# Attention layers of a two-layer kernel: the global layer's causal mask on GpSimd after the exponential, and five steps moved

## The chip, the cores and the metric

One core of one Trainium2 chip runs the whole program. The metric is the device time of one execution in microseconds (us); the kernel before took 745.13 us in the median of three runs (745.00 to 746.87). Engines are called as in the profile: PE is TensorE's matrix product (PEld its weight load), DVE is VectorE, ACT is ScalarE, POOL is GpSimd, SP is SyncE.

## The reference, cut to what matters

The input x is 8 sequences of 256 tokens of 128 numbers. Level 0 adds a two-directional Mamba block and a mixture of experts; level 1 adds an attention block and a second mixture of experts. The change lies in level 1's attention block, which is two layers one after the other:

```
x = x + global_latent_attn(rmsnorm(x, norm1_w), ...)   # causal mask
x = x + local_gqa_attn(rmsnorm(x, norm2_w), ...)       # causal, and within 32 tokens
# in each: 16 query heads, 4 key heads of 8 numbers; q, k rotated (rope), then
qk_norm(x) = x * rsqrt(mean(x * x, -1) + EPS)          # per head
scores = where(mask, q k^T / sqrt(8), -1e30); probs = softmax(scores); out = probs v
```

## The kernel before, in words

The program runs its stages one behind the other: level 0 to about 500 us, routing and experts of level 1 to about 565 us, then the attention stage (`attention_timeline`, lines 234 to 275) to the end at 742 us. Only that stage is touched.

**Units.** A sequence of one layer has three blocks of 128 keys by 128 queries, in the order `BLOCKS` = (0,0), (1,1), (0,1) as (key tile, query tile); a block is two units, each of two key heads, so that 16 sequence-layers give 96 units: 0 to 47 the global layer, 48 to 95 the local one. For a unit PE multiplies keys by queries into two PSUM banks (`scores`, L2133, or L2130 for the local corner blocks of 32 columns), ACT takes the exponential of 1024 columns into `probs` (`exps`, L1121), and once per block, two units, PE multiplies `probs` by the values (`average(t)`, L2160 or L2157). On the diagonal blocks (0,0) and (1,1) the mask is added on PE ahead of the scores: four 64-row products of an identity with a table of 0 and -30000 (L2122), which start the sum in PSUM. `scores(U)` waits until the exponential of unit U-2 has freed its banks; `probs` has three buffers.

**Preparation.** Tokens come in groups G of two sequences, four for each layer (G = 0 to 7), and a group is 12 units. Its steps are: rms (ACT squares L1031, DVE sum and variance L1481 and L1483, POOL's power -0.5 L702, DVE scaling L1489), T (PE transposes L1983, ACT copy L1034), L (latent product, global layer alone, L1978, ACT copy L1038), Q (PE L1989, DVE rotation L1543, L1545), K (PE L1987, DVE L1553 to L1565, the last of which writes `qk`), sqr (ACT squares `qk` L1042, DVE sum and variance L1570, L1574), inv (ACT logarithm and exponential L1045, L1048, DVE scaling L1577), split (ACT and DVE write float16 pairs, L1053, L1055, L1581, L1584), and behind the attention O1 and O2 (output transposes and product, ACT copy L1059, DVE sum L1588). Three turns for each sequence bring keys (part 0) and the two tiles of queries (parts 1 and 2) into the layout that the scores read: PE L2042 or L2048 into one bank, DVE copy L1625 or L1627. After its last average a sequence is copied by ACT (L1128), turned back by PE (L2168) and divided by its sums on DVE (`head_out`, L1659, L1665).

**Order.** Every engine runs its queue strictly in order, and all four queues are written from one list: `put(slot, event)` places an event at a slot number, one slot for each unit. PE's order in a slot is the events in the order of placing, then the unit, then the average. The others take turns, T, L and O1 first, then the unit, then the rest. The slots before the change are those of the removed lines of the diff; relative to 12G, and so modulo 12: Q 1, K 3, sqr 4, inv 5, split 6, rms 7, O1 7, O2 9, T 10, L 0; turns 9, 10, 0 and 3, 4, 6. POOL has nothing in this stage but the six powers.

Of the kernel before, what the change touches and what calls it, by code (L numbers as in the profile page):

```python
# [19 lines left out]
ALU = mybir.AluOpType  # L20
# [3 lines left out]
P = 128  # L24
# [77 lines left out]
    "turn_q", "turn_copied", "scores_ready", "probs_ready", "av_done", "den_done",  # L102
# [131 lines left out]
def attention_timeline():  # L234

    slots = {}

    def put(at, *ev):
        slots.setdefault(at, []).append(ev)

    for b in range(2 * SEQS):
        for part, at in enumerate((-3, -2, 0)):
            put(6 * b + at + (b == 0 and part == 2), "turn", b, part)
        put(6 * b + 10, "back", b)
        put(6 * b + 8, "copy", b)  # L260
    for G in range(GROUPS):
        for name, at in (("rms", -17), ("T", -14), ("L", -12), ("Q", -11), ("K", -9), ("sqr", -8), ("inv", -7), ("split", -6),
                         ("O1", 19), ("O2", 21)):
            if name != "L" or G < GROUPS // 2:
                put(12 * G + at, name, G)
    order, readers = [], []
    for at in range(min(slots), max(slots) + 1):
        here = slots.get(at, [])
        unit = [("unit", at)] if 0 <= at < UNITS1 else []
        if at % 2 and 1 < at <= UNITS1 + 1:  # L270
            unit.append(("average", at // 2 - 1))
        first = [ev for ev in here if ev[0] in ("turn", "T", "L", "O1")]
        order += here + unit
        readers += first + unit + [ev for ev in here if ev not in first]
    return order, readers
# [18 lines left out]
PREP = {ev: n for n, ev in enumerate(ev for ev in FILL + AT_ORDER if ev[0] in ("T", "L", "Q", "K", "O1", "O2"))}  # L294

# [73 lines left out]
def build(nc, a, out):  # L369
    with ExitStack() as ctx:  # L370
# [164 lines left out]
        def after(eng, name, count):  # L535

            if not (isinstance(count, int) and count <= 0):
                eng.wait_ge(sem[name], count)
# [109 lines left out]
        def _(pool):  # L648
# [135 lines left out]
            pool.memset(v_ring[:, :, :, :, VPAD + HD:VPAD + HD + 1], 1.0).then_inc(sem["ones_ready"], 1)  # L784
            for ev in FILL[1:] + AT_READERS:
                if ev[0] == "rms":
                    rms_pow(ev[1])


        @block.scalar  # L790
        def _(act):
# [226 lines left out]
            def prepare(ev):  # L1018
# [5 lines left out]
                if kind == "rms":  # L1024
# [14 lines left out]
                elif kind == "sqr":  # L1039
                    act.wait_ge(sem["roped"], G + 1)  # L1040
                    after(act, "qk_sum", G)
                    act.activation(qk_sqr[:], qk[:, r].rearrange("p h d -> p (h d)"), ACT.Square).then_inc(sem["qk_sq"], 1)  # L1042
# [97 lines left out]
        def _(dve):  # L1140
# [386 lines left out]
            def prepare(ev):  # L1527
# [8 lines left out]
                if kind == "rms":  # L1536
                    rms_sums(G)
                    rms_scale(G)
                elif kind == "Q":
# [27 lines left out]
                elif kind == "sqr":  # L1567
                    dve.wait_ge(sem["qk_sq"], G + 1)
# [114 lines left out]
        def _(pe):  # L1683
# [422 lines left out]
            def scores(U):  # L2106
# [8 lines left out]
                for kv in kvs:  # L2115
# [3 lines left out]
                    elif kt == qt:  # L2119
                        for rows in HALF_ROWS:  # L2120
                            keys = rows if kv == kvs[0] else HALF_ROWS[rows is HALF_ROWS[0]]
                            pe.matmul(ps[keys, kv], ident16[rows, rows],  # L2122
                                      masks[rows, l if kv == kvs[0] else 3 + l].unsqueeze(1).broadcast_to([P // 2, GROUP, P]),
                                      start=True, stop=False)
                if t % 3 < 2:
                    pe.wait_ge(sem["turn_copied"], TURN["turn", b, 1 + t % 3] + 1)
                for kv in kvs:
# [4 lines left out]
                    else:  # L2132
                        last = pe.matmul(ps[:, kv], kT[g, r, kt * P:(kt + 1) * P], qT[g, r, :, qt * P:(qt + 1) * P],  # L2133
                                         start=(kt != qt), stop=True)
                last.then_inc(sem["scores_ready"], 1)

            def average(t):
# [5 lines left out]
                pe.wait_ge(sem["probs_ready"], 2 * t + 2)  # L2143
                if t % 3 == 0:
                    pe.wait_ge(sem["v_ready"], b // 2 + 1)
# [125 lines left out]
```

## Time and profile before

| what | us |
|---|---|
| median of 3 runs | 745.13 |
| the profiled execution's own time | 744.09 |
| its span | 742.3 |
| attention stage, about 565 to 742.3 | 177 |
| ACT exponentials L1121, 96 | 86.5 busy |
| PE averages L2160, 640 products | 43.9 busy |
| POOL in the whole span | 418.6 busy, nearly all before 520 |

The page has the span in 40 slices of 18.6 us: in the attention stage PE is busy 8 or 9 tenths, ACT 6 or 7, DVE 5 or 6, POOL nothing to speak of. A busy PE is not PE at its peak, as its products overlap. Rows of the chain of waits are "start us, us, what"; rows of the timeline are "start us, duration us, engine, line, operation, output<-input, shapes, count", with idle time before the row and who ended it in brackets.

### The profile page before, as it was taken

How to read it: one execution, taken by the hardware profiler on the slowest of the kernel's cores; microseconds unless marked ns; L12 is line 12 of the kernel's file. 1: busy time of each engine (PE TensorE's matmuls, PEld its weight loads, DVE VectorE, ACT ScalarE, POOL GpSimd, SP SyncE). 2: the span in 40 equal slices, each digit the busy share in tenths (PEclk: the TensorE clock that was granted, in tenths of full speed). 3: DMA queues.
4: the chain of work that ended last, by engine and by line, in shares of the span. 5: the costliest groups of instructions: out<-in, count | busy, mean ns of one | idle time of the engine just before them, and what ended most of it. 6: DMA issues, size and time to landing. Idle time of an engine off the chain costs nothing.

```text
span 742.3 us, 14099 instructions
## 1 busy us (share of the span) xinstructions
PE 639.4 (86%) x4851; PEld 468.8 (63%) x4851; DVE 581.2 (78%) x852; ACT 526.4 (71%) x1001; POOL 418.6 (56%) x362
## 2 busy tenths in 40 slices
PE   5899987879889799798997985888999888989896
PEld 3488965657668577576675764876877344445443
DVE  6535769999999999999999999997316556566552
ACT  3455465896978969878789899673544777866673
POOL 5400047999999999999999999992000000000000
PEclk9699999999999999999999998999999999999998
DMA  6313467669688596885877858781110000000000
GB/s 210 114 58 115 147 145 219 208 160 262 182 201 252 158 239 198 183 253 169 193 260 157 250 181 195 228 230 43 57 58 1 2 1 1 2 1 2 15 16 29
DMA packets 81415, 100.18 MB, mean 135 GB/s; under 512 B 32561, under 2 KB 37817, under 8 KB 81345
## 3 DMA queue, kind: packets, MB, share of 16 engines
q1 hardware_dynamic: 81344, 99.29, 48.2%
q8 instruction: 39, 0.64, 0.3%
q14 instruction: 32, 0.25, 0.1%
HBM read 96.12 MB, written 3.24 MB: 134 GB/s over the span
## 4 chain that ended last, share of the span: by engine, by line
PE 50%; DVE 17%; issue 14%; ACT 13%; POOL 4%; DMA 0%; POOLq 0%; DVEq 0%; ACTq 0%
PE ps L1849 5%; DVE hc L1222 4%; DVE ps L1214 4%; PE ps L1827 3%; DVE moe L1214 3%; PE ps L2160 3%; PE ps L1904 3%; PE ps L1919 3%; PE ps L1759 2%; PE ps L1810 2%; PE ps L2133 2%; PE ps L2057 2%; PE ps L2067 2%; PE ps L1779 2%; POOL drive L689 2%
## 5 line engine op out<-in xcount | busy, mean ns | idle before, releaser
L689 POOL TENSOR_TENSOR drive<-dtu,b_sb 128x512 f32<-128x512 f32 x160 | 204.1, 1285 | 1.5 <-DMA b_sb<-bc_rows 1.4
L697 POOL TENSOR_TENSOR hc<-moe,c_sb 128x512 f32<-128x512 f32 x128 | 166.1, 1298 | 8.2 <-DVE moe L1214 8.2
L1214 DVE TENSOR_TENSOR_SCAN moe<-ps,drive 128x512 f32<-128x512 f32 x128 | 153.3, 1198 | 0.7 <-ACT decay_sb L885 0.5
L1849 PE MATMUL ps<-ident,hc 128*128 128x128 f32 x1024 | 134.9, 275 | 3.3 <-POOL hc L697 3.0
L1849 PEld LDWEIGHTS ps<-ident,hc 128*128 128x128 f32 x1024 | 116.6, 142 | 28.6 <-issue 19.3
L885 ACT ACTIVATE ps<-dt,negA 128x510 f32<-128x510 f32 x160 | 106.5, 677 | 28.9 <-DVE moe L1214 28.2
L1214 DVE TENSOR_TENSOR_SCAN ps<-decay_sb,ps 128x512 f32<-128x512 f32 x96 | 117.1, 1220 | 1.2 <-ACT decay_sb L885 1.1
L1121 ACT ACTIVATE probs<-ps 128x1024 f32<-128x1024 f32 (+1 forms) x96 | 86.5, 916 | 35.6 <-PE ps L2133 29.3
L702 POOL TENSOR_TENSOR stat<-stat,halfc 128x4 f32<-128x4 f32 x7 | 7.1, 1008 | 170.8 <-DVE stat L1483 170.8
L1222 DVE TENSOR_TENSOR hc<-ps,c_sb 128x512 f32<-128x512 f32 x128 | 85.2, 666 | 0.0
L885 ACT ACTIVATE decay_sb<-dt,negA 128x510 f32<-128x510 f32 x96 | 68.3, 711 | 16.0 <-DVE ps L1214 16.0
L1827 PE MATMUL ps<-xm,dtuT 128*128 128x128 f32 x384 | 53.1, 282 | 11.4 <-DVE hc L1222 11.4
L916 ACT ACTIVATE scaled<-dtuT,bT 128x128 f32<-128x128 f32 x192 | 60.0, 389 | 0.6 <-PE ps L1829 0.6
L1827 PEld LDWEIGHTS ps<-xm,dtuT 128*128 128x128 f32 x384 | 47.4, 194 | 15.3 <-issue 15.3
L1829 PE MATMUL ps<-ident,scaled 128*128 128x128 f32 x192 | 30.1, 280 | 27.9 <-DVE hc L1222 27.9
L1829 PEld LDWEIGHTS ps<-ident,scaled 128*128 128x128 f32 x192 | 21.9, 144 | 35.3 <-issue 26.2
L2160 PE MATMUL ps<-probs,v_all 128*32 128x256 f32 x640 | 43.9, 393 | 0.0
L1214 DVE TENSOR_TENSOR_SCAN ps<-ps,drive 128x512 f32<-128x512 f32 x32 | 39.1, 1222 | 2.0 <-ACT ps L885 2.0
L775 POOL TENSOR_TENSOR seqstat<-seqstat,halfc 128x2 f32<-128x2 f32 x8 | 5.6, 700 | 58.3 <-DVE seqstat L1412 58.3
L820 ACT ACTIVATE hT<-ps,wbuf 128x256 f32<-128x256 f32 x64 | 25.8, 476 | 16.2 <-PE ps L1904 16.2
L1627 DVE CAST qT<-ps 128x512 f16<-128x512 f32 x32 | 22.0, 689 | 17.3 <-PE ps L2048 17.1
L1919 PEld LDWEIGHTS ps<-wbuf,hT 128*128 128x128 f32 x256 | 30.8, 192 | 3.1 <-issue 2.5
(282 smaller groups left out, 1191.0 us busy)
## 6 DMA issues: line engine op xcount, KB each, us to landing
b_sb<-bc_rows SPq DMA_DIRECT2D x128, 256.0 KB, 4.2
c_sb<-bc_rows SPq DMA_DIRECT2D x128, 256.0 KB, 4.1
xm<-spot_rows SPq DMA_DIRECT2D x48, 256.0 KB, 4.9
wbuf<-in_pack SPq DMA_DIRECT2D x16, 514.0 KB, 3.5
wbuf<-in_pack SPq DMA_DIRECT2D x8, 512.0 KB, 5.5
spot_rows<-c_sb SPq DMA_DIRECT2D x6, 256.0 KB, 3.6
x_sb<-in_x SPq DMA_DIRECT2D x4, 256.0 KB, 3.8
out<-x_sb SPq DMA_DIRECT2D x4, 256.0 KB, 2.3
```

Source lines behind the costliest of these rows:

```text
L689: pool.tensor_tensor(drive_of(N, half), dtu[:, N // STATES % 2, half], b_sb[:, N % B_RING], ALU.mult) \
L697: pool.tensor_tensor(hc[:, 2 * (N % DEEP) + half], h_of(q), c_sb[:, N % C_RING], ALU.mult).then_inc(sem["hc_pooled"], 1)
L885: act.activation(seqs(decay_bank(q))[:, :, lo:lo + SEQ - 1], seqs(dt[:, g % 2, half])[:, :, lo:lo + SEQ - 1], ACT.Exp, scale=negA[:, g // ...
L916: last = act.activation(scaled[:, n % 2, block], dtuT[:, block], ACT.Copy, scale=bT[:, t, j:j + 1])
L1121: act.activation(probs[keys, t % 3, heads_u, 0:width], ps[keys, heads_u, 0:width], ACT.Exp, scale=HD ** -0.5).then_inc(sem["probs_ready"], 1)
L1214: dve.tensor_tensor_scan(h_of(q)[:, turn], decay_bank(q)[:, turn], source[:, turn], 0.0, ALU.mult, ALU.add).then_inc(sem["scan_done"], 1)
L1222: dve.tensor_tensor(hc[:, 2 * (N % DEEP)], h_of(q), c_sb[:, N % C_RING], ALU.mult).then_inc(sem["hc_ready"], 1)
L1827: last = pe.matmul(ps[:, H_BANKS[N % OWN_H], block], dtuT[:, block], spots[:, n % SPOT_RING, block], start=True, stop=True)
L1829: last = pe.transpose(ps[:, H_BANKS[N % OWN_H], block], scaled[:, n % 2, block], ident[:])
L1849: last = pe.matmul(ps[:, Y_BANK + half, block], hc[:, 2 * (N % DEEP) + half, block], ident[:], start=False, stop=True, is_transpose=True, ...
L1919: last = pe.matmul(bank[:, t * D:(t + 1) * D], hT[:, k, c, t * P:(t + 1) * P], wbuf[:, r, HIDDEN + CHUNKS + c * D:HIDDEN + CHUNKS + (c + 1 ...
L2160: last = pe.matmul(to, v, probs[:, t % 3, kv, pair * SEQ:(pair + 1) * SEQ], start=(t % 3 < 2 and pair == 0), stop=(t % 3 != 1 and pair == 1))
```

## The change

The causal mask of the global layer's diagonal blocks (32 units, `by_pool`) leaves PE; POOL instead zeroes the hidden entries of `probs` after the exponential, in place, with one `affine_select` over 128 x 1024 (`hide`), and `average` waits for a new signal, `probs_seen`. The local layer keeps its masks. `average(t)` comes one unit later (behind unit 2t+4 instead of 2t+3), and so the copy and turn back of a sequence (9 and 11 for 8 and 10), O1 and O2 (20 and 22 for 19 and 21). The third turn of a sequence comes one slot sooner (-1 for 0). For groups 2 to 7 rms becomes two events: squares, with the DVE sum and variance, at the old slot, and root, two slots later, in which ACT (logarithm, then exponential of -0.5 times it) computes what POOL's power did, and DVE scales; T comes one slot later (-13 for -14). The squares of `qk` (sqr) are taken by DVE, as a product of `qk` with itself, instead of by ACT.

```diff
-        for part, at in enumerate((-3, -2, 0)):
-            put(6 * b + at + (b == 0 and part == 2), "turn", b, part)
-        put(6 * b + 10, "back", b)
-        put(6 * b + 8, "copy", b)
+        for part, at in enumerate((-3, -2, -1)):
+            put(1 if (b, part) == (0, 2) else 6 * b + at, "turn", b, part)
+        put(6 * b + 11, "back", b)
+        put(6 * b + 9, "copy", b)
     for G in range(GROUPS):
-        for name, at in (("rms", -17), ("T", -14), ("L", -12), ("Q", -11), ("K", -9), ("sqr", -8), ("inv", -7), ("split", -6),
-                         ("O1", 19), ("O2", 21)):
+        for name, at in (("T", -13), ("L", -12), ("Q", -11), ("K", -9), ("sqr", -8), ("inv", -7), ("split", -6),
+                         ("O1", 20), ("O2", 22)):
             if name != "L" or G < GROUPS // 2:
                 put(12 * G + at, name, G)
+        if G >= 2:
+            put(12 * G - 17, "squares", G)
+            put(12 * G - 15, "root", G)
+        else:
+            put(12 * G - 17, "rms", G)
...
-        if at % 2 and 1 < at <= UNITS1 + 1:
-            unit.append(("average", at // 2 - 1))
+        if at % 2 == 0 and 2 < at <= UNITS1 + 2:
+            unit.append(("average", at // 2 - 2))
...
+def by_pool(U):
+    return U // 6 < SEQS and BLOCKS[U // 2 % 3] != (0, 1)
...
+            def hide(U):
+                pool.wait_ge(sem["probs_ready"], U + 1)
+                p = probs[:, U // 2 % 3, 2 * (U % 2):2 * (U % 2) + 2].rearrange("p g (j q) -> p g j q", j=GROUP)
+                pool.affine_select(p, p, [[0, 2], [0, GROUP], [1, P]], ALU.is_ge, 0.0, base=0, channel_multiplier=-1) \
+                    .then_inc(sem["probs_seen"], 1)
...
+                if kind == "root":
+                    act.wait_ge(sem["rms_var"], G)
+                    act.activation(stat[:, 1, rows], stat[:, 2, rows], ACT.Ln).then_inc(sem["rms_ln"], 1)
+                    act.wait_ge(sem["rms_ln"], G - 1)
+                    act.activation(stat[:, 3, rows], stat[:, 1, rows], ACT.Exp, scale=-0.5).then_inc(sem["rms_pow"], 1)
...
-                elif kind == "sqr":
-                    act.wait_ge(sem["roped"], G + 1)
-                    after(act, "qk_sum", G)
-                    act.activation(qk_sqr[:], qk[:, r].rearrange("p h d -> p (h d)"), ACT.Square).then_inc(sem["qk_sq"], 1)
...
                 elif kind == "sqr":
+                    dve.wait_ge(sem["roped"], G + 1)
+                    qk_row = qk[:, r].rearrange("p h d -> p (h d)")
+                    dve.tensor_tensor(qk_sqr[:], qk_row, qk_row, ALU.mult).then_inc(sem["qk_sq"], 1)
                     dve.wait_ge(sem["qk_sq"], G + 1)
...
-                    elif kt == qt:
+                    elif kt == qt and not by_pool(U):
...
-                                         start=(kt != qt), stop=True)
+                                         start=(kt != qt or by_pool(U)), stop=True)
...
                 pe.wait_ge(sem["probs_ready"], 2 * t + 2)
+                after(pe, "probs_seen", seen_before(2 * t + 2))
```

`seen_before(n)` counts the units below n that are POOL's.

## Rows read from the trace of the kernel before

**Rows 1.** Busy time by stretch, K product to K product (us, engines' busy time, PEclk, DMA).
```profile
591.93:614.69 22.76, 20.64 (x217) 10.27 (x215) 13.29 (x27) 17.28 (x24) 1.01 (x1) 1.00 0.01 1
614.69:636.56 21.87, 19.73 (x216) 10.31 (x214) 13.29 (x27) 16.67 (x23) 1.01 (x1) 1.00 0.01 2
636.56:658.22 21.66, 19.51 (x214) 10.08 (x213) 13.29 (x27) 16.59 (x23) 1.01 (x1) 1.00 0.01 1
658.22:680.00 21.78, 21.08 (x233) 11.91 (x231) 13.73 (x28) 15.41 (x24) 1.01 (x1) 0.92 0.01 2
```

**Rows 2.** Chain of waits, 604 to 615 us: start, us, engine, output, line.
```profile
604.38 1.02 POOL stat L702
...
607.10 0.66 PE ps L1983 x4
607.75 0.33 PE ps L2133 x4
608.08 1.00 PE ps L2160 x16
...
609.41 0.97 PE ps L1978 x2
...
611.06 1.16 PE ps L1989 x8
612.22 0.34 PE ps L2122 x4
...
614.76 1.03 PE ps L1987 x8
```

**Rows 3.** Timeline, one group from K to split, 592 to 602 us.
```profile
591.93 1.10 PE L1987 MATMUL ps<-w_kvu,latT 32*128 32x64 f32 x8
...
593.86 0.82 DVE L1565 TENSOR_TENSOR qk<-rot 128x640 f32<-128x640 f32 x1
...
596.53 0.49 DVE L1665 TENSOR_TENSOR moe<-ps,den 128x128 f32<-128x128 f32 x2
...
596.79 0.73 ACT L1042 ACTIVATE qk_sqr<-qk 128x640 f32<-128x640 f32 x1
...
597.55 0.82 DVE L1570 TENSOR_REDUCE norm<-qk_sqr 128x80 f32<-128x640 f32 x1 [0.53 <-ACT qk_sqr L1042]
...
598.64 0.27 ACT L1045 ACTIVATE norm<-norm 128x80 f32<-128x80 f32 x1 [0.21 <-DVE norm L1574]
...
599.24 0.82 DVE L1577 TENSOR_TENSOR qk<-qk,norm 128x640 f32<-128x640 f32 x1 [0.64 <-ACT norm L1048]
...
599.98 0.68 DVE L1627 CAST qT<-ps 128x512 f16<-128x512 f32 x1
...
600.42 1.04 ACT L1055 ACTIVATE qs<-qk 128x1024 f16<-128x1024 f32 x1
```

**Rows 4.** Timeline of ACT from the split to the second next exponentials.
```profile
601.37 0.58 ACT L1059 ACTIVATE xmT<-ps 128x512 f32<-128x512 f32 x1
...
602.75 0.63 ACT L1031 ACTIVATE sq<-xn 128x512 f32<-128x512 f32 x1
...
607.79 0.69 ACT L1034 ACTIVATE xmT<-ps,cols 128x512 f32<-128x512 f32 x1 [2.10 <-PE ps L1983]
...
608.38 1.93 ACT L1121 ACTIVATE probs<-ps 128x1024 f32<-128x1024 f32 x2
```

**Rows 5.** POOL by line and form: count, busy us, mean ns, idle before.
```profile
L689 POOL TENSOR_TENSOR drive<-dtu,b_sb 128x512 f32<-128x512 f32 x160 | 204.1, 1285 | 1.5 <-DMA b_sb<-bc_rows 1.4
...
L782 POOL MEMSET v_all<- 128x1040 f32 x1 | 1.0, 960 | 0.0
```

**Rows 6.** Timeline near 15 us, the program's start: DVE, then POOL.
```profile
13.01 0.69 DVE L1188 TENSOR_TENSOR xn<-xm,stat 128x512 f32<-128x512 f32 x1
...
15.58 1.75 DVE L1188 TENSOR_TENSOR xn<-xm,stat 128x512 f32<-128x512 f32 x1 [1.08 <-POOL stat L735]
...
15.51 1.27 POOL L670 TENSOR_TENSOR w_tap<-dtu,w_in 128x512 f32<-128x512 f32 x1
```

More of the change, by code:

```diff
@@ L101 @@
     "rope_a", "roped", "v_ready", "qk_sq", "qk_sum", "qk_var", "qk_ln", "qk_inv", "qk_normed", "qk_hi", "qk_split",
-    "turn_q", "turn_copied", "scores_ready", "probs_ready", "av_done", "den_done",
+    "turn_q", "turn_copied", "scores_ready", "probs_ready", "probs_seen", "rms_ln", "av_done", "den_done",
     "ones_ready", "av_copied", "av_turned", "heads_done", "out_ready",
@@ L294, with seen_before @@
 PREP = {ev: n for n, ev in enumerate(ev for ev in FILL + AT_ORDER if ev[0] in ("T", "L", "Q", "K", "O1", "O2"))}
+def by_pool(U):
+    return U // 6 < SEQS and BLOCKS[U // 2 % 3] != (0, 1)
+def seen_before(U):
+    return sum(by_pool(V) for V in range(U))
 def shared_before(q):
@@ L787, in _ @@
                     rms_pow(ev[1])
+                elif ev[0] == "unit" and by_pool(ev[1]):
+                    hide(ev[1])
         @block.scalar
@@ L1023, in prepare @@
                 rows = slice(GT * k, GT * k + GT)
-                if kind == "rms":
+                if kind == "root":
[3 more added lines that the diff above has]
+                    act.activation(stat[:, 3, rows], stat[:, 1, rows], ACT.Exp, scale=-0.5).then_inc(sem["rms_pow"], 1)
+                elif kind in ("rms", "squares"):
                     if l:
@@ L1538, in prepare @@
                     rms_scale(G)
+                elif kind == "squares":
+                    rms_sums(G)
+                elif kind == "root":
+                    rms_scale(G)
                 elif kind == "Q":
```

## The prediction, made before the changed kernel ran

> **What bounds the kernel now.** I read the page's slices first: the change touches nothing before about 565 us, so only the last 177 us count. Then I cut that stage by groups, from one K product to the next [rows 1]. A group takes 21.7 to 22.8 us, PE is busy in some 19.5 to 20.6 of them, ACT in 16.6 to 17.3, DVE in 13.3, POOL in 1.0. No engine fills the period. So I read the chain of waits [rows 2] and the timeline [rows 3, 4] to see how a group goes round, with the K product at 591.93 as zero:
>
> - K to norm: K product, DVE's rotation, whose last sum ends at +2.75; ACT squares `qk` only at +4.86, as its queue has exponentials ahead; DVE's sum follows at +5.62, ACT's logarithm at +6.71, DVE's scaling (L1577) ends at +8.13 [rows 3].
> - norm to T: ACT splits until +9.53, copies for O1, and squares the next group's tokens at +10.82 [rows 3, 4]; POOL's power ends at +13.47, DVE scales, copies keys and adds O2, and T starts at +15.17 [rows 2].
> - T to K: here PE is packed. Its rows follow each other without a gap to the next K product at +22.76 (614.69 in the window's bound) [rows 1, 2]: 7.59 us, three masks of 0.34 among them.
>
> The bound is therefore this ring through four in-order queues. PE alone sets only its last third.
>
> **Masks off PE.** 32 units lose four products each, 0.34 us a unit [rows 2]: 10.9 us of PE in all. Of the eight in a period of 12 units only the three between T and K lie on PE's packed stretch (1.0 us). The other five stand between K and T, where PE waits for ACT and DVE; there I cost them at nothing, since the split and the exponentials cover them. If that cover were gone, they would be worth 1.7 us a group.
>
> **Squares of `qk` on DVE.** Removed: 0.73 us of ACT. Added: one product over 640 elements with two SBUF inputs, as L1565, 0.82 us [rows 3]. DVE no longer waits for ACT's queue. Its queue from +2.75 is: copy of the second turn 0.6, squares 0.82, sum and variance 1.1 (598.64 less 597.55), copy of the third turn 0.6 (now ahead of the scaling, since that turn is a slot sooner), `head_out` 0.85 (reciprocal and the 0.49 row), scaling 0.82. That puts the scaling's end at about +7.47 for +8.13: a gain of 0.65. The logarithm and exponential are hidden behind the third turn's copy and `head_out`.
>
> **Root on ACT, two slots later.** Removed: POOL's 1.02 [rows 2] and DVE's wait for it. Added on ACT: two small operations of 0.27 each (as L1045), 0.57 with the handover. But they stand behind more of ACT's queue. From the scaling's end at +7.47: split to +8.79, exponential 0.93 (two took 1.93 less the overlap [rows 4]), squares 0.55, O1 copy 0.53, two exponentials 1.86, sequence copy 0.55, root 0.57: +13.8. Then DVE's scaling, a copy of the second turn and the O2 sum; in the old order scaling, key copy and O2 sum took 1.70 (607.10 less the power's end), here 1.97, as the turn's copy is 0.27 longer. T starts at +15.75 instead of +15.17. So moving the root costs what the faster norm gives, and 0.6 more; it is repaid because unit 10 and its average are by then already done.
>
> **T to K after the change.** T 0.58, unit 11; L must wait for T's copy, which ends 1.38 after T's start (607.79 + 0.69) [rows 4], since the average that used to lie between now comes behind unit 0: L at +1.43. Then L 0.97, unit 0 0.33, average 1.00, Q 1.09, units 1 and 2 side by side 0.33 (as the pair at 607.75), average 1.00, keys' turn 0.22, sum 6.37 for 7.59 [rows 2]. The period is 15.75 + 6.37 = 22.1 for 22.76: minus 0.65.
>
> **The sum without any contact between POOL and DVE.** First slots, two masks ahead of the first K: -0.7. K1 to K2 and K2 to K3: -0.65 each. K3 to K4 has no L, so Q waits for unit 0 and an average only: 15.75 + 4.87 = 20.6 for 21.87, -1.25. K4 to K5 ends in the local layer with its masks: 15.75 + 6.2 = 21.95 for 21.66, +0.3. The two local periods: +0.2 each. Behind the last K: -0.3. Together -2.8 us. The average, the copy and O1, O2 a unit later cost nothing more: behind unit 95 no unit follows, so PE's order of the last two averages is the same work.
>
> **POOL's selects, and what they meet.** The trace has no `affine_select`. Below lies the write-only row, 960 ns for 1040 elements; above lies twice the two-input row, 2.57 us for 1024 [rows 5]. I take 1.3 us: a select reads 1024 values from SBUF, as many as the two inputs of the 1285 ns row have together, and the read count is what separates those rows. Eight of them are 10 us of a 22 us period, so POOL keeps up; at 2.57 it would be 20.6 and just not. As latency they are hidden: `average` runs about two us after the second exponential of its block is done, and where a select ends later (unit 3's, at most 1.5 us) PE has slack between K and T. Queued behind that wait on PE are the next unit's scores, and ACT's exponential behind them.
>
> What is not hidden is contention. It shows at the start of the program [rows 6]: DVE's product over 512 elements with both inputs in SBUF takes 0.69 alone, and 1.75 when POOL's L670 (15.51 to 16.78) started 0.07 earlier: it stood until POOL was done and then took its 0.67. The ring has five such DVE steps between K and T on its critical side: rotation sum, the new squares, scaling of `qk`, key pairs, scaling of tokens; query pairs too. With POOL busy nearly 0.5 of the time I laid selects of length p beside the steps above, each side waiting for the other to finish: T comes later by 0.45 us for p = 1.0, 1.65 for p = 1.25, 3.25 for p = 1.5. A plain mean (busy share times half a select, over five to seven steps) gives 0.9, 1.4 and 2.0. I take +1.7 a period, in four periods with selects: +6.8.
>
> The Trainium skill, "SBUF — State Buffer", section "Who interferes with whom", says the same as a rule: a VectorE instruction with two SBUF inputs and a GpSimd one that reads SBUF exclude each other, the later one waiting in full. The 1.75 us row agrees [rows 6]. It speaks against this change, which adds both kinds. The skill's "GPSIMD Engine Reference", section "Performance pitfalls for Q7 kernels", gives compare-and-select loops 1.03 to 2.03 cycles an element; worked out at its 1.2 GHz that is an estimate of 0.88 to 1.73 us for a select, and by its two ends the sum would be near -2 or beyond +9 us; no row here shows it.
>
> **Forecast.** -2.8 + 6.8 = +4.0 on the profiled 744.09 (span 742.3 and 1.8 around it), so 748.1; the median lies 1.04 above the profiled run: 749.1.
>
> **Rivals.** (1) *The selects slip between DVE's steps* (short select, or phases that fall well): +0.45 x 4 - 2.8 = -1.0, no measurable change, 744.1. For it: DVE is busy in only 13.3 of 22.8 us [rows 1]. Against: selects become ready right behind exponentials, and DVE's steps come from the same ring. (2) *PE's relief counts in full.* If the masks outside T to K hold up ACT too, because scores wait for the exponential two units back and ACT then starves, the eight masks give 2.7 us a period and the first slots 0.7, less some contention: 4 x (-2.7 + 0.6) + 0.7 x -1 = about -9; half of it, -5, I take as its time: 740. For it: PE is busy for 20.6 of 22.76 us [rows 1]. Against: between K and T it is ACT and DVE that the chain follows. (3) *TensorE's clock.* In 658 to 680 the granted clock was 0.92 instead of 1.00 [rows 1], in a stretch where PE had lighter work than in the groups before, whose clock was full. The engine drops to its lower level (1.2 instead of 2.4 GHz) for part of that stretch. With masks gone the global groups grow light as well; a dip costs one to two us when it falls between T and K, four of them +6: 751. (4) *A select near 2.57 us*: POOL becomes the bound, periods go beyond 25 us, 758 or more. (5) *The mask leaves PE but the queue of PE waits in `average` instead*: every select is then on the path, the same 1.3 us that the 0.34 x 2 saved, +0.6 for each of 16 blocks, +10 less 3: 752; slack of two us speaks against it.
>
> **How the numbers follow.** Forecast, contention above the gain (747.5 to 753): 0.38; clock or waiting `average` on top, or the long select: 0.10; rival 1, within 0.3%: 0.20; rival 2 and anything faster: 0.32. 0.3% is 2.2 us, about what a measurement of this kernel tells from no change. That gives faster 0.32, within 0.20, slower 0.48. The range takes rival 2's middle at its low end and the long contention case at its high end: 739.5 to 756. The forecast's own range is 747.5 to 753.
>
> **What the profile of after would show.** Selects: their mean ns on POOL, and how many DVE rows of L1565, the new squares, L1577, L1581, L1489 are longer than 0.82, 0.82, 0.82, 0.42, 0.69. Right: several of them stretched by up to a select's length, periods K to K of 23 to 24 us in the global layer. Wrong by rival 1: durations as before, periods 22. Wrong by rival 2: periods near 20 and ACT idle for less than 4 us in each. The scaling L1577 should end about 7.5 us (plus contention) behind K, T start 15.75 or later, L wait for T's copy. A granted clock under 1.00 before 655 us would be rival 3, PE waiting for POOL ahead of L2160 rival 5.

## The result, and the profile after

The changed kernel took 750.92 us in the median of five runs (749.38 to 750.96), the kernel before beside it 745.0: a ratio of 1.0071 with a 95% interval of 1.0053 to 1.0090, so slower by more than 0.3%. The forecast of 749.1 had the sign and nearly the size. The profiled execution took 749.38, with a span of 747.7.

First the same cuts as [rows 1], from K product to K product, for the whole attention stage (us, then busy time of PE, PEld, DVE, ACT, POOL, then the mean granted clock, DMA share, GB/s):

```profile
571.45:595.39 23.94, 17.27 (x167) 8.33 (x167) 16.59 (x25) 15.88 (x24) 11.42 (x9) 0.86 0.00 1
595.39:617.60 22.21, 17.56 (x184) 9.20 (x182) 14.79 (x28) 16.80 (x25) 9.56 (x9) 1.00 0.01 1
617.60:638.97 21.37, 17.57 (x182) 9.72 (x181) 14.79 (x28) 16.42 (x24) 9.72 (x9) 0.92 0.01 2
638.97:663.18 24.21, 20.66 (x195) 11.69 (x195) 14.75 (x28) 16.74 (x24) 8.01 (x7) 0.86 0.01 1
663.18:684.88 21.70, 19.70 (x223) 11.41 (x222) 13.83 (x28) 13.52 (x24) 0.00 (x0) 0.92 0.00 1
684.88:707.59 22.71, 20.84 (x223) 11.85 (x222) 14.52 (x29) 14.13 (x24) 0.00 (x0) 0.85 0.05 13
707.59:747.70 40.11, 32.54 (x396) 17.73 (x394) 18.88 (x40) 22.50 (x34) 0.00 (x0) 0.94 0.07 21
```

The kernel before has seven such stretches too. Four of them [rows 1] do not hold, as the last window there, 658.22 to 680.00, is not from K to K. The third stands there with a bound of 636.56, where K starts at 636.39, so that it takes 21.70 us and not 21.87. These five are:

```profile
570.40:591.93 21.53, 18.39 (x200) 8.41 (x198) 13.95 (x24) 16.55 (x23) 1.01 (x1) 1.00 0.00 1
614.69:636.39 21.70, 19.56 (x214) 10.14 (x213) 13.29 (x27) 16.50 (x23) 1.01 (x1) 1.00 0.01 2
658.06:678.99 20.93, 20.23 (x222) 11.12 (x221) 13.31 (x27) 14.56 (x23) 1.01 (x1) 0.92 0.01 2
678.99:701.40 22.41, 20.47 (x223) 10.84 (x221) 13.91 (x28) 14.45 (x23) 1.01 (x1) 0.92 0.05 14
701.40:742.30 40.90, 33.47 (x396) 18.32 (x394) 18.27 (x39) 23.13 (x35) 0.00 (x0) 0.93 0.07 21
```

From the first K to the end: 176.1 us after, 171.9 before. The loss isn't spread as forecast. Two stretches carry it: the first, 23.94 for 21.53, and the fourth, 24.21 for some 21.7. The second is 0.55 us shorter than before (22.76 [rows 1]), the third 0.3 (21.70). And the granted clock, at its full 1.00 in the global layer before, is now 0.86, 0.92 and 0.86 in three of four stretches: TensorE ran for part of them at 1.2 instead of 2.4 GHz. A stretch of mean clock c holds half clock for 2 (1 - c) of its length. By that estimate it is about 27 us ahead of the last K against about 7 before (17 against 0 in the global layer's four stretches, 10 against 7 in the two local ones), and 32 against 13 with the last stretch.

Next, from the changed kernel's timeline, the cycle that begins with K at 595.39 (start, duration, engine, line, operation, shapes, idle time before and who ended it):

```profile
597.66 1.48 POOL L804 TENSOR_SCALAR_AFFINE_SELECT probs<-probs 128x1024 f32<-128x1024 f32 x1 [0.15 <-ACT probs L1146]
598.70 1.11 DVE L1599 TENSOR_TENSOR qk_sqr<-qk 128x640 f32<-128x640 f32 x1
...
602.21 0.81 DVE L1609 TENSOR_TENSOR qk<-qk,norm 128x640 f32<-128x640 f32 x1
...
607.25 0.38 PE L2080 MATMUL ps<-ident,qs 128*128 128x128 f16 x4 [1.48 <-DVE kT L1657]
...
609.01 0.99 DVE L1514 TENSOR_TENSOR xm<-xn,stat 128x512 f32<-128x512 f32 x1 [1.91 <-ACT stat L1052]
...
611.25 0.66 PE L2015 MATMUL ps<-ident,xm 128*128 128x128 f32 x4
```

The scaling of `qk` ends at +7.63 (forecast +7.47, plus contact), T starts at +15.86 (forecast +15.75), the next K comes at +22.21 (forecast 22.1 without contact, 23.8 with it). DVE's 1.91 us of waiting for ACT's root is the new wait that the later root was said to bring; PE stands idle for 1.48 us before the second turn. No wait of PE for POOL ahead of an average, the sign of rival 5, is in the trace.

Then the prices of contact, each line's instructions over the whole span (ns: shortest, median, longest):

```profile
L804 POOL TENSOR_SCALAR_AFFINE_SELECT probs<-probs x32: 1094/1097/3145, 569.9 to 651.9; 128x1024 f32<-128x1024 f32 x32
L1599 DVE TENSOR_TENSOR qk_sqr<-qk x8: 814/964/1111, 534.7 to 710.8; 128x640 f32<-128x640 f32 x8
L1613 DVE TENSOR_TENSOR ks<-qk,ks x8: 415/586/1012, 562.1 to 715.3; 128x256 f16<-128x256 f32 x8
L1514 DVE TENSOR_TENSOR xm<-acc,stat x4: 692/838/987, 631.2 to 698.1; 128x512 f32<-128x512 f32 x4
L1709 DVE TENSOR_TENSOR x_sb<-x_sb,sq x1: 3115/3115/3115, 571.6 to 571.6; 128x2048 f32<-128x2048 f32 x1
```

A select takes 1.10 us alone, not the 1.3 I took: it reads as many values as the two-input row of 1.28 us, so the read count alone does not set the length. It stretches the squares by 0.3 us, `ks` by up to 0.6, the token scaling by 0.3. The last row is a step that I had not looked at: the sum of the first residual, once, in the first cycle, 3.12 us for 2.28 before. What follows it in that cycle of the changed kernel:

```profile
571.52 5.82 POOL L804 TENSOR_SCALAR_AFFINE_SELECT probs<-probs 128x1024 f32<-128x1024 f32 x3 [0.49 <-ACT probs L1146]
571.64 3.12 DVE L1709 TENSOR_TENSOR x_sb<-x_sb,sq 128x2048 f32<-128x2048 f32 x1
...
577.14 0.38 PE L2080 MATMUL ps<-ident,qs 128*128 128x128 f16 x4 [2.94 <-DVE qT L1659]
```

Both sides wait: three selects take 5.82 us instead of 3.3, the sum 0.83 us more, and PE stands for 2.94 us before the third turn, whose predecessor's copy is queued behind the sum on DVE.

Last, PE in the fourth stretch, in the middle of a time at half clock:

```profile
651.16 2.02 PE L2021 MATMUL ps<-w_o,xmT 128*128 128x128 f32 x8
...
653.65 1.94 PE L2193 MATMUL ps<-probs,v_all 128*32 128x256 f32 x16
```

At full clock the same groups take 1.11 and 1.07 us: with the neighbours, some 2.4 us for this one dip (a dip is a time at half clock).

### The profile page after: what moved, and what is told of

It reads as the page before. It is cut to its first block, busy times and chain, and to the rows that moved or that the text cites. A ratio compares the mean times of both kernels' runs of the same rounds, so it can differ in the third digit from the quotient of the medians.

```text
span 747.7 us, 13951 instructions
## 1 busy us (share of the span) xinstructions
PE 632.3 (85%) x4723; PEld 468.9 (63%) x4723; DVE 590.9 (79%) x860; ACT 523.0 (70%) x1005; POOL 452.5 (61%) x388
## 4 chain that ended last, share of the span: by engine, by line
PE 52%; DVE 19%; issue 11%; ACT 11%; POOL 4%; SPq 1%; DMA 1%; DVEq 0%; POOLq 0%; ACTq 0%
PE ps L1881 6%; PE ps L2193 4%; DVE ps L1239 3%; PE ps L1936 3%; DVE hc L1247 3%; PE ps L1859 3%; PE ps L1951 3%; DVE moe L1239 3%; PE ps L2021 2%; PE ps L1791 2%; PE ps L1842 2%; POOL drive L704 2%; PE ps L2089 2%; PE ps L2099 2%; PE ps L1811 2%
## 5 line engine op out<-in xcount | busy, mean ns | idle before, releaser
L804 POOL TENSOR_SCALAR_AFFINE_SELECT probs<-probs 128x1024 f32<-128x1024 f32 x32 | 39.8, 1258 | 74.2 <-ACT probs L1146 74.1
L2193 PE MATMUL ps<-probs,v_all 128*32 128x256 f32 x640 | 46.3, 410 | 0.0
L2165 PE MATMUL ps<-qT,kT 32*128 32x512 f16 x160 | 28.9, 397 | 5.7 <-ACT probs L1146 4.2
```

The source lines that it names most:

```text
L2193: last = pe.matmul(to, v, probs[:, t % 3, kv, pair * SEQ:(pair + 1) * SEQ], start=(t % 3 < 2 and pair == 0), stop=(t % 3 != 1 and pair == 1))
```

## Experiments

The theory after the result: three things of different kinds add up. (a) The ring gains about what the no-contact sum said. (b) Contact with the selects takes back less than forecast. (c) The rest is half clock and the first cycle's sum. Rivals to it: contact alone; the order of the moved steps.

Diffs are against the changed kernel where nothing else is said.

### Parts of the change, undone or alone

**both_masks**: the masks stay on POOL, and TensorE adds them as well.

```diff
-                    elif kt == qt and not by_pool(U):
+                    elif kt == qt:
...
-                                         start=(kt != qt or by_pool(U)), stop=True)
+                                         start=(kt != qt), stop=True)
```

> The changed kernel with the four mask products of each diagonal block put back on PE as well, so that POOL still runs its 32 selects and PE has its old work. In the changed kernel's trace PE's clock stands at half for 27 us of the attention stage, in the kernel before for 7. If the clock is the cost, the global layer's dips go, and the time falls although PE has 10.9 us more to do: 746 to 748 against 750.9. If the contact of POOL with DVE is the cost, it stays or rises by what PE's added work takes: 751 to 754.

753.24 us, 1.0114 of before (1.0086 to 1.0143): 2.3 us over the change, with intervals that overlap by a little. The half clock ahead of the last K fell only from about 27 to 24 us, but not evenly: in the global layer, where the masks went back, from 17 to 10, while the local layer, whose work this edit leaves alone, had 14 for 10. So the mask products are partial cover, and they cost time of their own. That cost is read where the clock is full in both, in the second stretch:

```profile
595.83:619.64 23.81, 20.99 (x217) 10.42 (x215) 15.03 (x28) 16.94 (x25) 9.21 (x9) 1.00 0.01 1
```

It took 22.21 in the changed kernel: the relief of PE is worth 1.6 us there, of the 2.7 that eight masks are long.

**masks_back**: no selects at all, every mask by TensorE; the moved steps stay.

```diff
-    return U // 6 < SEQS and BLOCKS[U // 2 % 3] != (0, 1)
+    return False
```

> The changed kernel with all masks on PE and no select; every moved step stays moved. If POOL's contact with DVE or the lighter PE is the cost, this is at or under the kernel before: 742 to 746. If the moved steps are the cost (root behind two more exponentials, T a slot later), it stays at 749 to 751.

747.54 us, 1.0031 (1.0014 to 1.0048), between the two expected ranges. Four of its stretches:

```profile
595.30:618.20 22.90, 20.88 (x216) 10.41 (x214) 13.84 (x28) 16.79 (x25) 0.00 (x0) 1.00 0.01 1
639.60:660.90 21.30, 19.74 (x215) 10.26 (x213) 13.84 (x28) 16.14 (x24) 0.00 (x0) 1.00 0.00 1
660.90:683.30 22.40, 20.84 (x222) 11.56 (x221) 13.84 (x28) 13.44 (x24) 0.00 (x0) 0.85 0.01 1
683.30:706.50 23.20, 21.20 (x223) 12.29 (x221) 14.54 (x29) 14.19 (x24) 0.00 (x0) 0.85 0.05 13
```

The moved steps alone lose some 2.4 us, in two places. One is the first stretch, 23.3 for 21.5. The other is the local layer, where at a clock of 0.85 the two stretches take 22.4 and 23.2 for 20.9 and 22.4. The three global stretches in between, at full clock, take 22.9, 21.4 and 21.3 for 22.8, 21.7 and 21.7, and the last 39.8 for 40.9, which gives part of it back. With all masks on PE the global layer has about 3 us of half clock, all in the first stretch.

**masks_alone**: the kernel before, with the selects and with averages, copy, turn back, O1 and O2 a unit later; rms, T, third turn and squares as they were. The diff is against the kernel before and leaves out the selects, which are as in the change.

```diff
-        put(6 * b + 10, "back", b)
-        put(6 * b + 8, "copy", b)
+        put(6 * b + 11, "back", b)
+        put(6 * b + 9, "copy", b)
...
-                         ("O1", 19), ("O2", 21)):
+                         ("O1", 20), ("O2", 22)):
...
-        if at % 2 and 1 < at <= UNITS1 + 1:
-            unit.append(("average", at // 2 - 1))
+        if at % 2 == 0 and 2 < at <= UNITS1 + 2:
+            unit.append(("average", at // 2 - 2))
```

**old_root**: the changed kernel with masks by TensorE and rms and T in their old slots, with POOL's power.

```diff
-        for name, at in (("T", -13), ("L", -12), ("Q", -11), ("K", -9), ("sqr", -8), ("inv", -7), ("split", -6),
+        for name, at in (("rms", -17), ("T", -14), ("L", -12), ("Q", -11), ("K", -9), ("sqr", -8), ("inv", -7), ("split", -6),
...
-        if G >= 2:
-            put(12 * G - 17, "squares", G)
-            put(12 * G - 15, "root", G)
-        else:
-            put(12 * G - 17, "rms", G)
...
-    return U // 6 < SEQS and BLOCKS[U // 2 % 3] != (0, 1)
+    return False
```

> The kernel before with the masks by POOL and the averages, copies, turns back, O1 and O2 a unit later, nothing else moved. POOL's power then queues behind selects and DVE waits for it. If the masks part is the slow one: 750 or more. If the moved steps are: at or under the kernel before, 742 to 746.

> All masks on PE, no selects, and the rms steps back as they were: POOL's power in one event at the old slot, T at -14. What stays moved is the squares of qk on DVE, the third turn a slot sooner and the averages a unit later. By the ring of the prediction the norm comes 0.65 us a group sooner and the root's 0.6 us loss goes, so this is 743 to 745 and under masks_back (747.5) by 2 to 4 us. If the late averages are the cost, it stays at 747.

773.38 us, 1.0386 (1.0358 to 1.0413), and 774.37 us, 1.0384 (1.0370 to 1.0397); the second lies 27 us above anything that was expected. Both have periods of some 26 to 28 us as far as the last K. The timeline of old_root:

```profile
609.77 0.69 DVE L1509 TENSOR_TENSOR xm<-xn,stat 128x512 f32<-128x512 f32 x1 [1.12 <-POOL stat L712]
...
610.38 0.42 DVE L1652 CAST kT<-ps 128x256 f16<-128x256 f32 x1
...
610.95 0.59 PE L2075 MATMUL ps<-ident,qs 128*128 128x128 f16 x4 [2.95 <-DVE kT L1652]
...
611.33 2.02 PE L2016 MATMUL ps<-w_o,xmT 128*128 128x128 f32 x8
...
614.13 1.11 PE L2010 MATMUL ps<-ident,xm 128*128 128x128 f32 x4 [0.78 <-DVE acc L1615]
```

O2 a unit later falls into the slot of T at its old place (both in slot 10, modulo 12). DVE's key copy stands behind the scaling, which stands behind POOL's power; the second turn waits 2.95 us for it, and then O2, its sum and T follow one after the other at half clock (O2 2.02 us for 1.11). So the later root and T, moved together, are what makes the later averages possible at all: masks_back has them and takes 747.54. Which of the two it is, these runs don't part. The prediction took that move as costing 0.6 us, to be repaid; it had not seen what it prevents.

**squares_turn** (its diff is against the kernel before): the kernel before, with the squares of `qk` on DVE and the third turn a slot sooner.

```diff
-        for part, at in enumerate((-3, -2, 0)):
-            put(6 * b + at + (b == 0 and part == 2), "turn", b, part)
+        for part, at in enumerate((-3, -2, -1)):
+            put(1 if (b, part) == (0, 2) else 6 * b + at, "turn", b, part)
...
-                    act.activation(qk_sqr[:], qk[:, r].rearrange("p h d -> p (h d)"), ACT.Square).then_inc(sem["qk_sq"], 1)
...
+                    qk_row = qk[:, r].rearrange("p h d -> p (h d)")
+                    dve.tensor_tensor(qk_sqr[:], qk_row, qk_row, ALU.mult).then_inc(sem["qk_sq"], 1)
```

> The kernel before with two parts of the change alone: the squares of qk on DVE and the third turn a slot sooner. By the ring this is the gainful part: 0.65 us sooner in each of seven groups, 4 us at most, 741 to 743. If the order of the ring was read wrongly: 745.

751.43 us, 1.0072 (1.0059 to 1.0084), above both expected times. In its timeline, with K at 596.91:

```profile
600.10 0.39 PE L2047 MATMUL ps<-ident,qs 128*128 128x128 f16 x4
...
600.52 0.69 DVE L1626 CAST qT<-ps 128x512 f16<-128x512 f32 x1 [0.86 <-PE ps L2047]
...
601.92 0.82 DVE L1566 TENSOR_TENSOR qk_sqr<-qk 128x640 f32<-128x640 f32 x1
```

The squares start at +5.01, no sooner than ACT's at +4.86 [rows 3], and the scaling ends at +8.37 for +8.13. With the average still ahead of the second turn in PE's queue, DVE's copy waits for that turn and the squares wait behind the copy. In the changed kernel the average is later and the squares start at +3.31. So I read the 0.65 us a period that I gave to the squares' new engine as the work of that step and the late average together; no run has these two alone. Without the late average the two moves of this run lose 6 us. It isn't half clock: the global stretches behind the first take 23.2, 22.2 and 22.1 for 22.8, 21.7 and 21.7, all at 1.00.

### Contact

**write_only**: the select is replaced by a POOL operation that only writes; the mask of the global diagonal blocks is left out.

```diff
-                pool.affine_select(p, p, [[0, 2], [0, GROUP], [1, P]], ALU.is_ge, 0.0, base=0, channel_multiplier=-1) \
-                    .then_inc(sem["probs_seen"], 1)
+                if seen_before(U):
+                    pool.wait_ge(sem["probs_seen"], seen_before(U))
+                pool.memset(xnT[:, 0:1190], 0.0).then_inc(sem["probs_seen"], 1)
```

> The changed kernel with each select replaced by a fill of 1190 unused elements of SBUF, about as long (1.1 us) and waited for in the same way; it only writes, and the causal mask of the global layer is left out. If two readers exclude each other, DVE's rows are back at 0.82, 0.41 and 0.69 us, and the contact's price is what the time falls by: 1 us a group at most by the stretched rows, 4 to 5 us in all, 746 to 747. If the clock is the cost, dips stay and the time is 749 to 751.

748.52 us, 1.0054 (1.0030 to 1.0078), between the two expected ranges; that interval overlaps the change's. Its rows decide:

```profile
L1600 DVE TENSOR_TENSOR qk_sqr<-qk x8: 815/815/824, 533.1 to 705.1; 128x640 f32<-128x640 f32 x8
L1614 DVE TENSOR_TENSOR ks<-qk,ks x8: 415/426/426, 560.6 to 709.6; 128x256 f16<-128x256 f32 x8
L1710 DVE TENSOR_TENSOR x_sb<-x_sb,sq x1: 2282/2282/2282, 570.1 to 570.1; 128x2048 f32<-128x2048 f32 x1
```

Every stretched row is back at its own length, though POOL is busy for 8.7 us of a stretch (9.6 with selects). The stretch comes from a POOL operation that reads. The dips stayed: about 21 us of half clock in the global layer of the profiled execution, which was the fastest of the twelve (744.87), so contact doesn't cause them. Its second stretch is at full clock:

```profile
592.53:614.13 21.60, 17.55 (x185) 9.21 (x183) 13.84 (x28) 16.76 (x25) 8.73 (x9) 1.00 0.01 2
```

Between it and the 22.9 us of masks_back lie only the masks on PE and an operation on POOL that stretches nothing: without contact the relief is worth 1.3 us. And about 3 us of half clock in the global layer with masks (masks_back) against 21 without (write_only) says what brings most dips there: the masks' leaving. The mean clock over the whole span, 0.965 and 0.954 in the median of twelve executions each, agrees.

**add_late**: the changed kernel with the first residual's sum at unit 12 instead of 3. By then part of `sq` is overwritten, so the residual isn't the reference's.

```diff
-                elif ev == ("unit", 3):
+                elif ev == ("unit", 12):
```

> The changed kernel with DVE's 128 x 2048 sum into x_sb (3.12 us against 2.28 before, as POOL's select held it) moved from unit 3 to unit 12, where DVE waits 3.2 us for Q. The first period took 23.9 us against 21.5 before, with PE idle for 2.9 us behind that sum and half clock after it. If that sum is the cause of the first period, it falls to 21 to 22 us and the time by 1.5 to 3 us, to 748 to 749.5. If not, no change.

748.29 us, 1.0026 (1.0006 to 1.0047). The first stretch is 21.4 us instead of 23.9, at the same low clock (0.84 for 0.86), and the time is 2.6 us less: the sum is what lengthened that stretch.

**before_split** and **masks_back_split** move it without changing the result, in the kernel before and in masks_back: rows 8 to 12 at unit 3, the others at unit 12.

```diff
-                    dve.tensor_tensor(x_sb[:], x_sb[:], sq[:], ALU.add).then_inc(sem["x1_ready"], 1)
+                    dve.tensor_tensor(x_sb[:, 8:12], x_sb[:, 8:12], sq[:, 8:12], ALU.add).then_inc(sem["x1_ready"], 1)
+                elif ev == ("unit", 12):
+                    dve.tensor_tensor(x_sb[:, 12:16], x_sb[:, 12:16], sq[:, 12:16], ALU.add).then_inc(sem["x1_ready"], 1)
+                    dve.tensor_tensor(x_sb[:, 0:8], x_sb[:, 0:8], sq[:, 0:8], ALU.add).then_inc(sem["x1_ready"], 1)
```

> The kernel before with VectorE's addition of the first residual (2.28 us in front of the copy for the second turn in the first cycle) split: rows 8 to 12 of it at unit 3, the others at unit 12. If the in-order queue of VectorE hands this instruction to the first period one for one, the first K to K is 1.1 to 1.7 us shorter than its 21.5 and the time is 743 to 744. If the first period is set by the loads and weights, nothing moves: 745.

> The changed kernel with every mask by TensorE again (no select at all), and the same split of VectorE's addition. With all masks by TensorE and the addition whole it was 1.0031 of the kernel before. If the addition is what the moved steps lose, 745 to 746 us. If it is the dips or the order, 747 to 748 as it was.

745.04 us, 0.9987 (0.9972 to 1.0002), and 746.35 us, 1.0004 (0.9983 to 1.0024). Where the moved steps stand, the first stretch falls from 23.3 to 22.2 us; the two local ones stay at a clock of 0.85 and 22.5 and 23.2 us. In the kernel before it doesn't fall (21.7 for 21.5), so there the sum was hidden, and splitting it makes no faster kernel. The split run of before gives the price of a dip, as its order behind the first cycle is unchanged:

```profile
661.80:682.70 20.90, 18.97 (x223) 10.38 (x221) 13.30 (x27) 14.43 (x23) 1.01 (x1) 1.00 0.01 2
682.70:703.60 20.90, 18.96 (x223) 10.38 (x221) 13.91 (x28) 14.42 (x23) 1.01 (x1) 1.00 0.05 15
```

With a clock of 0.92 the kernel before took 20.93 and 22.41 for these two: the same mean clock cost nothing in one and 1.5 us in the other. It matters where the dip lies. And since the order is the same, dips also come and go from one execution of a kernel to the next; what one profile counts of them is one sample.

### The clock

**keep_busy**: seven needless products behind the scores of unit 9.

```diff
+                    if ev[1] % 12 == 9 and ev[1] < 12 * (GROUPS - 1):
+                        keep_busy(n)
```

> The changed kernel with seven needless products of 512 columns (0.21 us each) on PE behind the scores of unit 9 of every group of twelve, where PE stands idle for 1.3 to 1.5 us in each group before the second turn. They write the preparation bank before O2 or T overwrites it, and take nothing that another engine waits for. In the changed kernel half clock follows each such idle stretch (582 to 590, 630 to 634, 650 to 658 us). If the clock is what the missing masks cost, half-clock time goes from 27 us to under 10 and the time to 745 to 748. If the clock doesn't matter, 750 to 753.

750.44 us, 1.0058 (1.0040 to 1.0077), the time that was expected if the clock didn't matter. But the edit didn't do what it was for:

```profile
608.81 3.17 PE L2209 MATMUL ps<-masks,ident 128*128 128x512 f16 x7 [0.62 <-ACT xmT L1084]
```

The products wait for O1's copy, last 3.17 us and outrun the gap, and the half clock still is about 17 us ahead of the last K. So the run decides nothing about the clock.

**fill_gaps** puts them at two places, into banks that are free at that time (in this run `keep_busy(n, bank, count)` issues `count` products of the masks' first tile with the identity; `filled` is true for units below 84):

```diff
+                    if ev[1] % 12 == 9 and filled:
+                        keep_busy(n, AV_BANK + 1, 3)
...
+                    if ev[1] % 12 == 7 and filled:
+                        keep_busy(n, PREP_BANK, 5)
+                    if ev[1] % 12 == 9 and filled:
+                        keep_busy(n, AV_BANK + 1, 6)
```

> The changed kernel with products put into TensorE's idle stretches of every unit cycle but the last: five behind the scores of unit 7, three before and six behind those of unit 9, all of the masks' first tile with the identity, into banks that nobody reads then. If the stretches at half clock are what is left of the loss (27 us of them in the profiled run of the changed kernel, some 2.4 us for one of 6.8 us), the profile shows under 10 us of them behind the first K, periods of 21.3 to 22 us, and 745 to 747 us. If order and contact alone set the time, the products bring nothing or delay the unit behind them: 751 or more, with the dips or without.

745.72 us, 0.9998 (0.9983 to 1.0014). Its stretches:

```profile
571.00:594.00 23.00, 20.10 (x181) 9.03 (x181) 16.58 (x25) 15.87 (x23) 11.47 (x9) 0.85 0.00 1
594.00:616.20 22.20, 20.79 (x198) 10.29 (x197) 14.80 (x28) 16.79 (x25) 9.56 (x9) 1.00 0.01 1
616.20:636.80 20.60, 19.64 (x196) 10.22 (x195) 14.79 (x28) 16.43 (x24) 9.77 (x9) 1.00 0.01 2
636.80:658.60 21.80, 21.11 (x208) 10.70 (x207) 14.76 (x28) 16.56 (x24) 7.94 (x7) 1.00 0.01 2
658.60:679.80 21.20, 21.20 (x237) 11.69 (x237) 13.84 (x28) 13.54 (x24) 0.00 (x0) 1.00 0.01 2
679.80:700.90 21.10, 21.10 (x236) 11.58 (x235) 14.53 (x29) 14.09 (x24) 0.00 (x0) 1.00 0.05 14
700.90:743.60 42.70, 36.06 (x410) 19.67 (x409) 18.89 (x40) 22.69 (x35) 0.00 (x0) 0.92 0.07 20
```

All that was added is useless work in TensorE's queue, 14 products in each of seven cycles, 24.7 us of PE's busy time in all, and the kernel got 5 us faster. From the second stretch to the sixth the clock is 1.00 throughout; the third, fourth, fifth and sixth are shorter than in the changed kernel by 0.8, 2.4, 0.5 and 1.6 us. The selects' and DVE's rows are the same (DVE busy 14.80 for 14.79), so neither contact nor the order of the real work moved. The second stretch is the control: its clock was full without the products too, and it takes 22.2 us with them and without. The first keeps its mean clock (0.85 for 0.86) and is still 0.9 us shorter: its half clock now lies at 574 to 580 us, where PE stood waiting anyway, and no longer at 583 to 589. The products behind the last K lengthen the last stretch, 42.7 for 40.1. Other executions say the same as the profiled one: the mean clock over the whole span is 0.952 to 0.967 in five runs of the changed kernel, 0.958 in the median, and 0.971 in the median of twelve here.

**write_fill**: the same products, and the write-only operation in place of the select; the mask of the global diagonal blocks is left out. Its edit is the two diffs of write_only and fill_gaps together.

> The same products, and the select in place of a write-only memset of 1190 elements of another buffer (the upper half of the diagonal probabilities is not cut to zero, so part of the computation is left out). Contact and dips would both be gone: if these two are the whole loss, 742 to 745 us, VectorE's squares at 0.82 us and its ks at 0.43. If the order of the steps itself costs, it stays at or over 747.

743.21 us, 0.9954 (0.9940 to 0.9968), with an interval apart from that of fill_gaps; the two have the same clock in every stretch shown:

```profile
571.30:593.50 22.20, 20.25 (x180) 9.06 (x180) 14.56 (x25) 15.93 (x24) 8.73 (x9) 0.85 0.01 1
593.50:615.10 21.60, 20.60 (x198) 10.32 (x196) 13.84 (x28) 16.76 (x25) 8.74 (x9) 1.00 0.01 2
615.10:635.10 20.00, 19.46 (x197) 10.24 (x195) 13.84 (x28) 16.40 (x24) 8.96 (x9) 1.00 0.01 2
635.10:656.40 21.30, 20.97 (x209) 10.81 (x207) 13.84 (x28) 16.57 (x24) 7.41 (x7) 1.00 0.01 2
```

Contact is the difference of the two: DVE busy 0.96 us less in the second and third stretch, the stretches 0.8, 0.6, 0.6 and 0.5 shorter, 2.5 us in all.

## Why the prediction came out right, point by point

It had the sign and nearly the size, but by two errors that cancel: contact was priced too high, and half clock stood in the sum at nothing. That the time fell into the range is in that part luck. The sum in its own terms:

| term | forecast | measured, from |
|---|---|---|
| ahead of the first K | -0.7 | not resolved: K at 570.4 before, 571.5 after, but 573.9 in before_split, whose order is the same up to there |
| four periods, no contact | -2.25 | -2.6 (write_fill 85.1 us, before 87.7) |
| contact, four periods | +6.8 | +2.5 (fill_gaps less write_fill) |
| half clock | none; rival 3, +6 | about +5 net (the change less fill_gaps), +6.2 from first to last K, ahead of the 2.5 that the products cost behind it |
| two local periods | +0.2 each | +0.2 each (fill_gaps 21.14, before_split 20.92, at full clock) |
| behind the last K | -0.3 | -0.8 |

In the profiled executions these add up. The first K comes 1.05 us later. From there to the last K write_fill takes 3.7 us less than the kernel before (2.6 in the four periods, the rest in local ones, where before had dips of its own), contact adds 2.6, half clock 6.2. Behind the last K 0.8 is gained. Together that is +5.4, from 742.3 to 747.7.

- **The ring was right.** That K, norm, T and K go round through four in-order queues, and that no engine's busy share sets the period, is shown by the timeline (+7.63, +15.86, +22.21). The no-contact periods at full clock are 21.6, 20.0 and 21.3, each 0.5 to 0.7 below the forecast of 22.1, 20.6 and 21.95.
- **The relief was mis-sized.** The prediction counted three of eight masks, 1.0 us a period, and put the other five at nothing. Where the clock is full the eight were worth 1.3 us (masks_back less write_only) to 1.6 (both_masks less the change): about half of their 2.7.
- **The no-contact sum agrees by luck as well.** Its four periods came out at +0.7, -1.2, -1.8 and -0.4 us for -0.65, -0.65, -1.25 and +0.3. The first gained nothing, as the first cycle has its own long instruction and a dip.
- **Small slips in the working.** The third period before is 21.70 and not 21.87, so its term should be -1.1. DVE's queue adds up to +7.54 and not +7.47. In [rows 6] DVE's product took 0.55 us after POOL was done (16.78 to 17.33) and not 0.67, so that some 0.14 us of it ran ahead of the wait; in the changed kernel's cycle it is the same (`qk_sqr` ends 0.67 us after the select, for 0.82). None of them moves the forecast.
- **But the parts don't stand alone.** The prediction gave 0.65 us a period to the squares on DVE. squares_turn shows no such gain in the old order; masks_alone and old_root lose 28 us without the later root and T. The sum was right for the whole set of moves only.
- **The contact term was mis-sized**, 1.7 us a period for 0.6. Its mechanism holds in full (write_only, write_fill). Two steps failed: the select's length (1.3 us, for which the two-input row stood model; measured 1.10), and the way from stretched rows to the period. DVE's rows do grow by 0.95 us a period, but with 14.8 of 22.2 us busy DVE has slack, and a third of that growth never reaches the next K. My own table gave 0.45 us for a select of 1.0 and 1.65 for one of 1.25, about 0.9 for the real 1.10, so the size hung on the second digit of an unknown price.
- **The sum of the first residual** was left out of the five DVE steps: 0.83 us of the longest contact there is, and on the path in the first cycle. The step that failed is the ring itself, read in one cycle only and taken for all; the first cycle has a DVE instruction between K and T that the others lack.
- **Half clock was a term of nothing in the sum**, priced only as a rival (751, within a chance of 0.10), and it was the largest part of the loss. The evidence was in [rows 1]: 0.92 in the local layer, whose work on PE is lighter. I read that as something that may happen to the global layer, and not as a cost whose chance should be high once PE's busy time falls from 20.6 to 17.6 us of a period. What I missed is where PE would then stand idle, as in the 1.48 us before the second turn.
- **Rival 2** (relief counts in full, chance 0.32) fell: about half of PE's relief went into its idle time. **Rival 4** (a select of 2.57) fell by the 1097 ns row, **rival 5** by PE's waits. **Rival 1** is nearly what fill_gaps shows: with contact at its measured 0.6 a period and 7 us of half clock ahead of the last K the change is worth nothing, 0.9998.

The Trainium skill's rule that was weighed, in "SBUF — State Buffer", section "Who interferes with whom", agrees with these runs, for an in-place select as for a product (`qk_sqr` 1.11 us beside a select, 0.82 alone), and for an operation that only writes too (nothing was stretched in write_only). What a stretched row costs the period had to be measured.

Open: what exactly in PE's work calls the dips. That they cost the 5 us is shown by fill_gaps, and that the masks' leaving brings those of the global layer by masks_back against write_only. Why masks added back beside the selects (both_masks) removed only some of them, and why the moved steps have more in the local layer (14 us in masks_back and in masks_back_split, 7 and 0 in before and before_split), is not shown. These counts are from one profiled execution each. Nor did I run the fills in the kernel before, or in the changed kernel without those behind the last K, which lengthen its last stretch by 2.5 us. No kernel that computes the reference was measurably faster than the kernel before.

## What to carry to other kernels

Work taken off TensorE is gain only where the period waits for it, here about half of it; and it can cost, where the idle time that it leaves ends in half clock. Look at the granted clock stretch by stretch, and if it falls after a relief, try needless products into free banks at the idle places. That tells clock from order, if the trace shows that they fill the gap and the clock rises (fill_gaps did, keep_busy didn't). Where GpSimd gets a reading operation beside DVE's two-input ones, price it by the few DVE rows on the ring, expect a part of their stretch in the period (here two thirds), and search every cycle, the first too, for a long DVE instruction that a select can hold up.

## What the runs showed of the hardware that I had not expected

- An in-place `affine_select` over 128 x 1024 float32 takes 1.10 us on GpSimd, less than its two-input product over half as many elements (1.28 us [rows 5]).
- A mean clock of 0.92 in a stretch cost 0 or 1.5 us, in two neighbouring stretches of the kernel before that take 20.90 us each at full clock.
- Needless products on TensorE, 98 of them with 24.7 us of its busy time, brought back 5 us of 751.
